# Decoder layer with a mixture of experts: fewer small VectorE instructions in the batch loop, and x transposed in 32x32 squares

## The reference

```python
# x, ctx: (32, 128, 128) f32: 32 batches of 128 tokens with 128 features; 16 heads of 8
def layernorm(x): return (x - mean(x)) / sqrt(var(x) + 1e-5)
def attn(x):                         # causal linear attention
    q, k, v = split(x @ qkv_w.T + qkv_b); q = relu(q) + 1e-6; k = relu(k) + 1e-6
    kv = cumsum(einsum('bhld,bhle->bhlde', k, v), axis=2)
    num = einsum('bhld,bhlde->bhle', q, kv); den = max(q . cumsum(k), 1e-6)
    return (num / den) @ out_w.T + out_b
def xattn(x, c):                     # 16 heads, window |i-j| <= 64, keys = values = ctx
    return softmax(mask(q @ k.T / sqrt(8))) @ v @ W_proj.T + b_proj
def ffn(x):                          # top-1 of 8 experts, capacity 641 tokens each
    scores = softmax(x @ wg); top1 = argmax(scores); gate = scores[top1]
    rank = how many tokens before this one chose the same expert
    slot = top1 * capacity + rank    # if rank < capacity; the rest get 0
    h = gelu(buf[slot] @ W1[e] + b1[e]); y = h @ W2[e] + b2[e]
    return y * gate
x = layernorm(x + attn(x)); x = layernorm(x + xattn(x, ctx)); x = layernorm(x + ffn(x))
```

## Time and profile before

| | us |
|---|---|
| median of three runs | 418.44 |
| the runs | 419.33, 415.81, 418.44 |
| the profiled execution | 417.75 |
| its span in the profile | 416.0 |

### The profile page before, as it was taken

How to read it: one execution, slowest core, us unless ns; L and a number is a source line. 1 busy time by engine, 2 the same in 40 slices (tenths; PEclk the granted TensorE clock), 3 DMA queues, 4 the chain that set the end, 5 groups by cost and what they waited for, 6 DMA issues and landing times.

```text
span 416.0 us, 19194 instructions
## 1 busy us (share of the span) xinstructions
PE 389.4 (94%) x7065; PEld 294.6 (71%) x7065; DVE 328.2 (79%) x1645; ACT 268.7 (65%) x609; POOL 252.6 (61%) x372
## 2 busy tenths in 40 slices
PE   7989999999999999999999999998878999999970
PEld 6647777777777777777777767766566788888860
DVE  6366688988889888888988988977875478877880
ACT  4536777777877677787778777776756544445560
POOL 5344455676676676666677667476564037777683
PEclk9999999999999999999999999999998999999995
DMA  3900000111201010111111114000011566666100
GB/s 110 321 26 17 23 23 16 29 28 30 57 27 30 28 29 28 43 42 29 28 31 28 38 35 135 9 24 14 17 50 49 141 126 149 153 146 165 52 30 15
DMA packets 44674, 24.69 MB, mean 59 GB/s; under 512 B 19417, under 2 KB 40719, under 8 KB 44582
## 3 DMA queue, kind: packets, MB, share of 16 engines
q1 hardware_dynamic: 42246, 19.27, 17.7%
q0 software_dynamic: 2336, 4.20, 3.1%
HBM read 14.43 MB, written 9.58 MB: 58 GB/s over the span
## 4 chain that ended last, share of the span: by engine, by line
PE 82%; issue 5%; POOL 4%; DVE 2%; DMA 2%; ACT 2%; SPq 1%; POOLq 1%; DVEq 0%; ACTq 0%
PE banks L789 13%; PE banks L739 13%; PE banks L1214 9%; PE banks L1200 8%; PE banks L731 8%; PE banks L751 7%; PE banks L724 6%; PE banks L801 3%; PE banks L868 2%; PE banks L817 2%; PE banks L769 2%; PE banks L770 2%; PE banks L771 2%; PE banks L912 1%; POOL expert_in L520 1%
## 5 line engine op out<-in xcount | busy, mean ns | idle before, releaser
L1730 DVE TENSOR_REDUCE mx<-banks 128x8 f32<-128x1024 f32 x64 | 77.0, 1219 | 19.5 <-PE banks L739 19.5
L1278 ACT ACTIVATE arena<-banks 128x1024 f32<-128x1024 f32 x64 | 62.1, 1021 | 41.1 <-PE banks L739 41.1
L789 PEld LDWEIGHTS banks<-arena,V 128*32 128x32 f32 x2048 | 53.1, 109 | 29.8 <-ACT arena L1308 23.6
L789 PE MATMUL banks<-arena,V 128*32 128x128 f32 x2048 | 67.0, 275 | 0.6 <-ACT arena L1308 0.3
L1308 ACT ACTIVATE arena<-banks 128x1024 f32<-128x1024 f32 x64 | 62.1, 1022 | 6.0 <-PE banks L731 6.0
L1531 ACT ACTIVATE arena<-banks,b1T 128x321 f32<-128x321 f32 x64 | 33.8, 528 | 39.4 <-PE banks L1200 38.7
L487 POOL TENSOR_TENSOR rs<-ve,minus_half 128x1 f32<-128x1 f32 x32 | 18.1, 567 | 54.7 <-DVE ve L1698 54.7
L656 POOL DMA_INDIRECT out_x<-ot,idx x40 | 40.3, 1007 | 18.1 <-issue 9.0
L504 POOL TENSOR_TENSOR rs<-ve,minus_half 128x2 f32<-128x2 f32 x32 | 23.2, 725 | 38.6 <-DVE ve L1718 38.5
L520 POOL DMA_INDIRECT expert_in<-x,sidx x32 | 35.2, 1099 | 16.6 <-DVE x L1804 5.6
L1214 PEld LDWEIGHTS banks<-w_sb,arena 128*128 128x128 f32 x320 | 37.7, 192 | 3.1 <-issue 1.8
(11 more groups left out here) (216 smaller groups left out, 968.7 us busy)
## 6 DMA issues: line engine op xcount, KB each, us to landing
w_sb<-in_L_ffn_W SPq DMA_DIRECT2D x16, 256.0 KB, 3.2
EB<-expert_in SPq DMA_DIRECT2D x9, 325.0 KB, 4.8
expert_in<-zeros SPq DMA_DIRECT2D x10, 266.5 KB, 3.3
X<-in_x SPq DMA_DIRECT2D x32, 64.0 KB, 1.9
C<-in_ctx SPq DMA_DIRECT2D x32, 64.0 KB, 2.8
out_x<-fb SPq DMA_DIRECT2D x32, 64.0 KB, 2.1
EQ<-expert_in SPq DMA_DIRECT2D x24, 80.0 KB
out_x<-ot,idx POOLq DMA_INDIRECT x40, 2.2
```

Source lines behind the costliest of these rows:

```text
L789: mm = pe.matmul(bank(name)[VW * s:VW * (s + 1), half * P:(half + 1) * P], V[:, h, :], scored[:, h // NA, h % NA, :], start=q == 0, stop=q ...
L1278: nc.scalar.activation(A1[b % 2][:, 2 * half:2 * half + 2].rearrange("p j a t -> p j (a t)"), pair("s1", half), ACT.Relu).then_inc(s1_out[ ...
L1730: v.tensor_reduce(mx[b % 2][:, 8 * half:8 * half + 8].rearrange("p (j a) -> p j a", a=NA), pair("s2", half).rearrange("p j (a t) -> p j a ...
```

## The change

In the batch loop, four edits on small instructions and one on the transpose of x:

- `op_ve2`: one instruction on two columns, scale x variance + shift with constants in two small tiles, in place of two.
- `slot0` goes from `op_rk1`; `op_rk3` computes `slot1` as -656 x top + rank in one instruction, as before from `slot0` and rank, and the constant is added where `slot1` is used (`sidx`, `minus_slot`, `op_hot`).
- The increment of the token number moves from `op_rk4` on VectorE to `op_x2` on POOL.
- For batches 4 to 31 `load` also brings x in 32x32 squares to `XQ`, a ring of four tiles, by four DMAs, so that the transpose of each square gives `xT`. `op_xT` of these batches goes from TensorE, and `op_xTe` is VectorE's transpose of `XQ` in place of the copy from PSUM. `X` itself is still loaded, for the residual.

```diff
+    SQ = 4
+    SLOT0 = float(E * CAPP - 1)
...
+            def squares(to, rows, arrived):
+
+                view = rows.rearrange("(k j) d -> j k d", j=VW)
+                for q in range(G):
+                    sp.dma_start(to[VW * q:VW * (q + 1), :].rearrange("j (k i) -> j k i", i=VW),
+                                 view[:, :, VW * q:VW * (q + 1)]).then_inc(arrived, 16)
+
             def load(b):
                 k = b % RX
-                wait(sp, xT_full, b - RX + 1)
+                wait(sp, xT_full, min(b - RX + 1, SQ))
...
                 sp.dma_start(C[k][:], ctx_in[b]).then_inc(x_in[k], 16)
+                if b >= SQ:
+                    if b >= 2 * SQ:
+                        sp.wait_ge(xT_done, b - SQ + 1)
+                    squares(XQ[b % SQ], x[b], xq_in[b % SQ])
...
                 wait(pool, scattered[b % 4], 16 * (b // 4))
+                if b >= 4:
+                    token = x2[b % 4][:, TOKEN:TOKEN + 1]
+                    g.tensor_scalar(token, token, float(4 * P), None, ALU.add)
                 g.tensor_scalar(x2[b % 4][:, 0:D], r2[:], mv2[:, 0:1], rs2[:, 0:1], ALU.subtract, ALU.mult).then_inc(x2_ready, 1)
...
             def op_xT(b):
+                if b >= SQ:
+                    return
...
+            for k, (scale, shift) in enumerate([(1.0, LN_EPS), (1.0 + LN_EPS, LN_EPS * LN_EPS)]):
+                v.memset(ve_scale[:, k:k + 1], scale)
+                v.memset(ve_shift[:, k:k + 1], shift)
...
-                v.tensor_scalar(ve2[:, 0:1], mv2[:, 1:2], LN_EPS, None, ALU.add)
-                v.tensor_scalar(ve2[:, 1:2], mv2[:, 1:2], 1.0 + LN_EPS, LN_EPS * LN_EPS, ALU.mult, ALU.add).then_inc(
-                    var2_ready, 1)
+                v.scalar_tensor_tensor(out=ve2[:], in0=ve_scale[:], scalar=mv2[:, 1:2], in1=ve_shift[:], op0=ALU.mult,
+                                       op1=ALU.add).then_inc(var2_ready, 1)
...
-                v.tensor_scalar(slot0[:], top[k][:], -float(CAPP), float(E * CAPP - 1), ALU.mult, ALU.add)
...
-                v.tensor_scalar(slot1[:], slot0[:], rank[b % 2][:], None, ALU.add).then_inc(slot1_ready, 1)
+                v.scalar_tensor_tensor(out=slot1[:], in0=top[b % 2][:], scalar=-float(CAPP), in1=rank[b % 2][:], op0=ALU.mult,
+                                       op1=ALU.add).then_inc(slot1_ready, 1)
...
-                v.tensor_scalar(sidx[b % 4][:], slot1[:], over[:], None, ALU.add)
+                v.tensor_scalar(sidx[b % 4][:], slot1[:], over[:], SLOT0, ALU.add, ALU.add)
...
-                if b >= 4:
-                    token = x2[b % 4][:, TOKEN:TOKEN + 1]
-                    v.tensor_scalar(token, token, float(4 * P), None, ALU.add)
...
             def op_xTe(b):
-                dve.wait_ge(xT_full, b + 1)
                 wait(dve, qkv_full, b - 1)
-                copied(xT[b % 2], "xT", xT_done)
+                if b < SQ:
+                    dve.wait_ge(xT_full, b + 1)
+                    copied(xT[b % 2], "xT", xT_done)
+                else:
+                    dve.wait_ge(xq_in[b % SQ], 16 * G * (b // SQ))
+                    v.transpose(xT[b % 2][:], XQ[b % SQ][:]).then_inc(xT_done, 1)
```

More of the change, by code:

```diff
@@ L144, in decoder @@
         xb = ring("xb", 4, [P, D])
+        XQ = ring("XQ", SQ, [P, P])
         xT = ring("xT", 2, [P, P])
@@ L179, in decoder @@
         ve2 = sb("ve2", [P, 2])
+        ve_scale = sb("ve_scale", [P, 2])
+        ve_shift = sb("ve_shift", [P, 2])
         rs2 = sb("rs2", [P, 2])
@@ L197, in decoder @@
         rank = ring("rank", 2, [P, 1])
-        slot0 = sb("slot0", [P, 1])
         slot1 = sb("slot1", [P, 1])
@@ L265, in decoder @@
         x_in = [sem(f"x_in{k}") for k in range(RX)]
+        xq_in = [sem(f"xq_in{k}") for k in range(SQ)]
         consts = sem("consts")
@@ L1797, in op_rk4 @@
                 wait(dve, scattered[b % 4], 16 * (b // 4))
-                v.tensor_scalar(sidx[b % 4][:], slot1[:], over[:], None, ALU.add)
+                v.tensor_scalar(sidx[b % 4][:], slot1[:], over[:], SLOT0, ALU.add, ALU.add)
                 if LATE <= b < B - 1:
-                    v.tensor_scalar(minus_slot[:, b - LATE:b - LATE + 1], slot1[:], 1.0 if b == LATE else -1.0, None, ALU.mult)
-                if b >= 4:
-                    token = x2[b % 4][:, TOKEN:TOKEN + 1]
-                    v.tensor_scalar(token, token, float(4 * P), None, ALU.add)
+                    sign = 1.0 if b == LATE else -1.0
+                    v.tensor_scalar(minus_slot[:, b - LATE:b - LATE + 1], slot1[:], sign, sign * SLOT0, ALU.mult, ALU.add)
                 v.tensor_scalar(x2[b % 4][:, GATE:GATE + 1], rank[b % 2][:], float(CAP), rsum[:], ALU.is_le, ALU.mult).then_inc(slot_ready, 1)
@@ L1837, in op_hot @@
                 r0, r1 = HALVES[half]
-                v.tensor_scalar(hot[B - 1 - LATE][:, r0:r1], slot_of[:, r0:r1], slot1[:], None, ALU.is_equal).then_inc(hot_last, 1)
+                v.tensor_scalar(hot[B - 1 - LATE][:, r0:r1], slot_of[:, r0:r1], slot1[:], SLOT0, ALU.subtract,
+                                ALU.is_equal).then_inc(hot_last, 1)
             op_xTe(0)
```

## The result

The changed kernel takes **419.55 us** (median of 11 runs, 419.33 to 423.93) against 418.24 us (11 runs, 415.73 to 419.86) for the kernel before: a ratio of 1.0064, 95% interval 1.0033 to 1.0094. It is slower, by some 0.3 to 0.9%. I had forecast 417.8 us and a small gain; the time lies in my range and on the wrong side of zero. In a second comparison it took 420.84 us (12 runs) against 417.74 (33 runs), ratio 1.006 (1.0029 to 1.0091).

What follows compares the result with a forecast made beforehand. The prediction took TensorE to bound the batch loop. Its terms, 0 - 0.4 + 0.5 - 0.3 = -0.2 us against the profiled 417.75, gave 417.55; it forecast 417.8 us, between that and the median-based level, range 413.9 to 421.

Steps and rivals of the forecast that it cites:

- The transpose is worth 0: Batch loop on TensorE: removing x's transpose gives 0, as the fourth mask still waits for x2T's evacuation.
- my upper bound of 2.9: TensorE's transpose of x: the most its removal could give, 26 transposes at 0.11 us, 2.9 us.
- Late batches, -0.4: Every second loop batch, x2 late for TensorE: -1.2 us there, pauses moving elsewhere, net -0.4 (-1.2 to +0.5).
- one `ve2` shortens the chain by 0.07: VectorE's part of the x2 chain: one instruction in place of two makes it 0.07 us shorter.
- The token, 0 per batch: POOL, ahead of x2 in the loop: 0.2 us less 0.07 fits the 0.21 slack, so 0 per batch.
- The drain's +0.5: Last batches, where x2 has no slack: four tokens on POOL cost 4 x (0.2 - 0.07) = +0.5 us.
- Fewer VectorE operations, -0.3: slot0 and token leave VectorE: becomes waiting in the loop, gains -0.3 us in the drain (0 to -0.8).
- The replacement on VectorE, 0: VectorE's square transpose instead of the PSUM copy: 0.28 us, same as now, so 0; at most 0.21 more per batch.
- SyncE and DMA, 0: Four more DMAs per batch, 0.5 us each to issue: the squares have 17 us to land, so 0.
- the squares hold SyncE's queue: Rival, chance 0.04: square loads come late or hold SyncE's queue, 0.5 us per batch, 430 us.
- The token is dear: Rival, chance 0.10: POOL's token costs up to 0.567 us, exceeding x2's slack in loop and drain, 424.4 us.
- the first rival: Rival, chance 0.18: removing TensorE's transpose pays in full, 2.9 us plus 1.2 from late batches, 413.7 us.

Runs made afterwards that it cites:

- before_sq: Kernel before with only the square loads of x and its VectorE transpose added, two fb tiles: 418.01 us, ratio 1.0009.
- after_fb4_tokv_slot: Changed kernel with four fb tiles instead of two, the token back on VectorE, and slot0 and a tensor_scalar slot1 restored: 416.76 us, ratio 0.9956.
- second profile of after: Changed kernel run again unaltered; the profiled execution took 419.64 us, and the median of its 12 runs was 420.84 us.
- best_mask: after_fb4_tokv_slot with the four s1 masks of the fourth bank moved behind the other twelve: 415.68 us, ratio 0.9957.
- best_bank6: after_fb4_tokv_slot with x2's transpose written to bank 6 instead of bank 5: 413.39 us, ratio 0.9893.
- before_fb4_bank: Kernel before with four fb tiles and x2's transpose written to bank 7 instead of bank 5: 433.12 us, ratio 1.0362.
- first profile of after: Changed kernel as first profiled, without further edits; that execution took 423.93 us.

## Why the prediction was wrong, step by step

- **The transpose is worth 0: right in size, and right in its reason for the squares alone.** The loop keeps its length within 0.3 us with and without it (178.1 against 178.4 in the kernel before, 178.5 against 178.8 with the other edits). With the token on VectorE the fourth mask waits for x2T's bank, as I had said. In the changed kernel the second mask waits for VectorE's maxima in its place, at the same price. With x2T's claim gone and the token on VectorE the transpose is worth 416.01 - 413.39 = 2.6 us of the time, and 1.7 + 0.2 of the stages up to batch 24, under my upper bound of 2.9.
- **Late batches, -0.4: right in sign, too small.** The alternation is gone (it is still there in before_sq, with periods of 8.62 and 9.31 us, and not in after_fb4_tokv_slot). With the token on VectorE the loop is 0.9 us shorter (177.5 against 178.4). The steps of it are 0.3 each, with the squares (178.1), with one `ve2` and the base moved to `sidx` (177.8) and without `slot0` (177.5), hardly more than the spread of a stage. But "one `ve2` shortens the chain by 0.07" was wrong: one scalar_tensor_tensor takes 217 ns, and the two before took 0.07 + 0.146 = 0.22 from start to end. A count of instructions is not a length.
- **The token, 0 per batch: wrong.** Its price was 0.245 us, against 0.2 taken. Without the 0.07, which did not come, 0.245 stood against a slack of 0.21, so 0.035 per batch: over 24 batches 0.8. That fits the 0.6 to 1.0 measured in the loop. It ate the gain of the late batches. That it would also make VectorE's `rcoh` 0.19 us longer was in none of my terms. The drain's +0.5 lies between +0.1 and +0.9 in the profiles, the higher with 10.2 us at 1.2 GHz in it, and is not settled.
- **Fewer VectorE operations, -0.3: the sign right, the place wrong.** I expected the gain in the drain and nothing in the loop. `slot0` alone is worth 0.3 to 0.9 us in the loop, in three pairs. The drain shows no gain. The fold also gave `slot1` a second tile as input, and with it a stall of 1.5 us in one place, worth at most 1 us of the time.
- **The replacement on VectorE, 0: right.** 300 ns for the square transpose, 0.28 taken, and nothing waited for it.
- **SyncE and DMA, 0: this is the step that failed.** Issue was priced well (median 0.43 us each, 0.5 taken), and VectorE never waited for a square. But "behind them on its queue is only the store of `fb`, whose buffer ScalarE wants again long after" rested on one pair of rows, from the steady loop: 13 us. At 238.40 us, where the end of the loop has its own order, the same pair in the profile of before is 3.4 us apart, with a wait of 0.8 already in it. Four issues more there put the store 1.9 us later and made it 3.0 to 3.3 us, and 2.9 us of the time. The store's landing, 3.3 to 3.8 us with a block of instructions ahead of its last packets, was in no term either.

The sum of before to the second profile of after: loop -0.03 (-0.9 all edits but the token, +0.8 the token), batches 20 to 24 +3.2 (the store, and less than 1 us for the stall), drain 0, rest -1.1 by the clock (the low stretch lay ahead of batch 31 there), start -0.2: 1.9 us, as the spans say (417.9 against 416.0).

Of the rivals, *the squares hold SyncE's queue* was the true one, at one place and at 3 us, not in each batch and at 12. *The token is dear* is true in kind (x2T late in each batch) and small in size. (Its own sum is 5.3 + 4 x 0.37 = 6.8, not 6.6, and the first rival's 413.7 lies just outside the range that I said takes in most of it; neither moves anything.) Of the list of what would show it, the spread of the masks and the periods near 8.9 came as under "right", though the spread had the second mask at its head; x2T late by POOL came as under "wrong". That the time fell inside the range is luck in part: the loss of 2.9 us stood in none of its terms, and the range was wide for the transpose and the clock.

Open: the worth of the stall on `slot1`, and the token in the drain. That the last 8 packets of the store queue behind an instruction block is inferred from their times in nine profiles, not tested. And the new bank was tried only with the token on VectorE; what it gives where VectorE's maxima hold the second mask is not known.

## What to carry to other kernels

Slack read in the steady loop holds for the steady loop alone: for each thing that is put on a queue, look up the tightest reuse of every buffer behind it over the whole program, above all where the order is written by hand, and give that ring one more tile first. If removing work from a full engine does nothing, look for the claim that the next instruction waits on; freeing it (here one number in a table of banks) took 416.76 us to 413.39, while the removal alone was worth 0. Judge edits of this size by the length of a stage in the profiles, since the whole time moves by more than that from run to run.

## What the runs showed of the hardware

- **The clock sets the levels of the time.** The rest behind batch 31 takes 96.2 to 96.3 us in profiles where no stretch of 1.2 GHz lies in it ahead of the last, 97.3 where 1.6 us of one does, 99.4 to 99.5 with 6.8 us, and 100.9 with 9.2. Half of the low time, about, is lost. These stretches begin at 308 to 331 us, where TensorE has waited in the drain; the profiles of best_mask, best_bank6 and before_fb4_bank have none there. The first profile of after has one more at 244.3 us, behind the wait for the store.
- **One operation can wait for two of another engine.** `slot1` started 0.01 us ahead of POOL's xb in the records, and ended with the QE behind it, 1.49 us long instead of 0.15. `rcoh` is 0.34 us long where it starts 0.12 us behind POOL's x2, and 0.15 where it starts 0.35 behind.
- **Masks in one row group follow one another at 0.06 us**, and four groups run side by side: the 16 start within 0.19 us where nothing holds them (best_bank6), and within 0.31 where the last group starts 0.13 late, in either order (best_mask, after_fb4_tokv_slot).
- **A store can wait for instructions.** With a 16 KB block on a DMA engine ahead of its last 8 packets the store of fb takes 3.0 to 3.8 us, without 1.6 to 2.0 (five and four profiles; that they share the engine is inferred).
- **VectorE's operations of one column** start 0.07 us apart though each is recorded with 0.14, and the `ve2` of 217 ns in place of two of them shortened nothing.
